# A recurrent mixing in log space: numerator, denominator and reciprocal replaced by a running mean with sigmoid weights

## What is computed

```
def step(carry, kv_t):
    p, q, o = carry
    no = maximum(o, u + kt);  A = exp(o - no);  E = exp(u + kt - no)
    y = (A * p + E * vt) / (A * q + E)
    no2 = maximum(w + o, kt); A2 = exp(w + o - no2); E2 = exp(kt - no2)
    return (A2 * p + E2 * vt, A2 * q + E2, no2), y
```

## Time and profile before

| | us |
|---|---|
| median of 3 runs | 2321.01 |
| lowest and highest | 2313.25, 2324.97 |
| profiled execution | 2336.95 |
| its span | 2335.2 |

### The profile page before, as it was taken

How to read it: one execution, slowest core, us unless ns; L and a number is a source line. 1 busy time by engine, 2 the same in 40 slices (tenths; PEclk the granted TensorE clock), 3 DMA queues, 4 the chain that set the end, 5 groups by cost and what they waited for, 6 DMA issues and landing times. The chain is left out here.

```text
span 2335.2 us, 36369 instructions
## 1 busy us (share of the span) xinstructions
PE 1755.0 (75%) x9338; PEld 1261.9 (54%) x9338; DVE 1225.8 (52%) x3526; ACT 762.4 (33%) x2164; POOL 1033.9 (44%) x1023
## 2 busy tenths in 40 slices
PE   7989946775569999999985655552177888888883
PEld 3566633443247777777753332322167677777762
DVE  3123343543334466666668777775334456666664
ACT  3312212111024454545443232222033333344341
POOL 5040043465713333333320566656655555555552
PEclk9989977887779999999996766665589999999996
DMA  9756557652246788776430263325745566777774
GB/s 304 215 125 159 145 179 260 256 175 79 99 146 224 250 277 284 282 278 226 150 138 27 98 238 110 107 92 192 265 133 149 150 204 226 236 239 239 242 241 175
DMA packets 244106, 444.72 MB, mean 190 GB/s; under 512 B 92561, under 2 KB 174609, under 8 KB 241169
## 3 DMA queue, kind: packets, MB, share of 16 engines
q1 hardware_dynamic: 168352, 237.46, 32.1%
q0 software_dynamic: 47856, 147.81, 17.7%
q10 hardware_dynamic: 27712, 57.28, 7.3%
HBM read 281.09 MB, written 237.60 MB: 222 GB/s over the span
## 5 line engine op out<-in xcount | busy, mean ns | idle before, releaser
L1041 PE MATMUL ps<-w_all,h_xT 128*128 x2112 | 557.2, 387 | 32.1 <-ACT h_xT L1312 21.1
L792 POOL DMA_INDIRECT y_b<-h_y,h_ix x314 | 313.3, 998 | 271.0 <-DVE h_y L1874 178.7
L1058 PE MATMUL ps<-w_all,h_hT 89*128 (+1 forms) x1472 | 413.1, 385 | 11.2 <-issue 6.1
L1041 PEld LDWEIGHTS ps<-w_all,h_xT 128*128 128x128 f32 x2112 | 346.8, 193 | 89.6 <-issue 42.9
L776 POOL DMA_INDIRECT xs_b<-h_x,slot_of x256 | 263.9, 1031 | 237.5 <-DVE slot_of L1705 162.0
L792 POOL DMA_INDIRECT y_a<-h_y,h_ix x208 | 201.6, 969 | 349.4 <-ACT h_y L1345 334.7
L1058 PEld LDWEIGHTS ps<-w_all,h_hT 89*128 89x128 f32 (+1 forms) x1472 | 269.1, 191 | 82.0 <-issue 26.8
L776 POOL DMA_INDIRECT xs_a<-h_x,slot_of x192 | 191.0, 995 | 194.1 <-DVE slot_of L1705 92.5
L1312 ACT COPY h_xT<-ps 128x256 f32<-128x256 f32 x528 | 195.0, 370 | 131.9 <-PE ps L1034 89.9
L1049 PE MATMUL ps<-ident,h_h 128*88 128x128 f32 (+1 forms) x736 | 170.1, 277 | 70.6 <-DVE h_h L1867 59.5
L1867 DVE TENSOR_TENSOR h_h<-ps,h_sg 128x96 f32<-128x96 f32 x320 | 81.8, 256 | 229.3 <-ACT h_sg L1322 198.6
(11 more groups left out here) (257 smaller groups left out, 2442.4 us busy)
## 6 DMA issues: line engine op xcount, KB each, us to landing
xs_b<-void_d SPq DMA_DIRECT2D x40, 1128.0 KB
h_x<-xs_b SPq DMA_DIRECT2D x80, 564.0 KB
h_c<-y_a ACTq DMA_DIRECT2D x28, 768.0 KB
h_x<-xs_a SPq DMA_DIRECT2D x34, 564.0 KB, 4.7
xs_a<-void_d ACTq DMA_DIRECT2D x16, 1128.0 KB
w_all<-in_exp SPq DMA_DIRECT2D x6, 2560.0 KB
h_x<-y_b SPq DMA_DIRECT2D x28, 512.0 KB
s_b<-y_b SPq DMA_DIRECT2D x28, 512.0 KB
```

The source lines that it names most:

```text
L792: pool.indirect_dma_start(y_d[L.name], bass.IndirectOffsetOnAxis(ap=h_ix[:, i % IX:i % IX + 1], axis=0), result_buffer(L, i), None).then_i ...
L1041: m = pe.matmul(ps[:, 2 + s % 2, 0:2 * L.H], h_xT[:, s % 2, c, :], w_all[:, bass.ds(e * L.W + c * 2 * L.H, 2 * L.H)], start=(c == 0), stop ...
L1058: m = pe.matmul(ps[:, 6 + s % 2, 0:D], h_hT[0:w, s % 2, j, :], w_all[0:w, bass.ds(e * L.W + L.up0 + j * D, D)], start=(j == 0), stop=(j == ...
```

## The change

The mixing is rewritten. With the logarithm of the running denominator, L = ln(q) + o, the mean m = p / q obeys m' = s m + (1 - s) v, with s the sigmoid of (w + L - k), and y = m + (v - m) sigmoid(u + k - L). The sigmoids are written as halves of 1 + tanh. The new lists:

- VectorE: `largest` is the scan of `w_o` alone, both halves at the head of the turn; `weight_sums` is the scan of the denominator `w_q`, both halves behind `residual`; `mixed` makes the keep factor `w_keep` by a tensor_scalar, `w_ev`, one scan `w_p`, and three more operations up to `w_y`. `w_max`, the two reciprocals, and the last multiplication are gone.
- ScalarE: two exponentials a half instead of four, then a logarithm of `w_q` a half (`logarithms`), and two tanh a half (`shares`), those of half 0 behind `rows_normalised`, those of half 1 behind `turned`.
- TensorE: two differences a half of two products, and one of three (`past_less_key`), which waits for the logarithm.
- Buffers of the stage grow by 44 floats per partition. The DMAs and the lists of SyncE and GpSimd are the same.

```
 PE
-            def differences(g, c):
...
+            def difference(n, plus, less):
+                if n >= 3:
+                    pe.wait_ge(wk_exp, n - 2)
+                for i, a in enumerate(plus):
+                    pe.matmul(ps[:, spread[n % 3], :], ident[:], a, start=(i == 0), stop=False)
+                pe.matmul(ps[:, spread[n % 3], :], minus[:], less, start=False, stop=True).then_inc(wk_less, 1)
+            def decays_of(g, c):
                 pe.wait_ge(wk_t, 2 * g + c + 1)
+                difference(6 * g + 2 * c, [w_o[:, c, :, 0:SEQ]], w_o[:, c, :, 1:SEQ + 1])
+                difference(6 * g + 2 * c + 1, [w_k[:, c, :, 1:SEQ + 1]], w_o[:, c, :, 1:SEQ + 1])
+            def past_less_key(g, c):
+                pe.wait_ge(wk_ln, 2 * g + c + 1)
+                difference(6 * g + 4 + c, [w_o[:, c, :, 0:SEQ], w_l[:, c, :, 0:SEQ]], w_k[:, c, :, 1:SEQ + 1])
...
-                    differences(g, 0)
-                    differences(g, 1)
+                    decays_of(g, 0)
+                    decays_of(g, 1)
+                    past_less_key(g, 0)
+                    past_less_key(g, 1)
 ACT
+            def logarithms(g, c):
+                act.wait_ge(wk_q, 2 * g + c + 1)
+                act.activation(w_l[:, c], w_q[:, c], ACT.Ln).then_inc(wk_ln, 1)
+            def shares(g, c):
+                src = of_bank(6 * g + 4 + c)
+                act.activation(w_tau[:, c, 1], src, ACT.Tanh, bias=w_half[:, c:c + 1], scale=0.5).then_inc(wk_tau, 1)
+                act.activation(w_tau[:, c, 0], src, ACT.Tanh, bias=w_half[:, KC + c:KC + c + 1], scale=0.5)\
+                   .then_inc(wk_exp, 1)
...
+                    logarithms(g, 0)
+                    logarithms(g, 1)
                 if g:
                     deviations(L1, g - 1)
                     rows_normalised(g - 1)
...
+                    shares(g, 0)
                     turned(L1, g - 1)
+                    shares(g, 1)
                     exponentials_of(L1, g - 1)
 DVE
+            def largest(g, c):
...
+                dve.tensor_tensor_scan(flat(w_o[:, c]), flat(w_dec[:, c]), flat(w_k[:, c]), 0.0, ALU.add, ALU.max)\
+                   .then_inc(wk_t, 1)
+            def weight_sums(g, c):
+                dve.drain()
+                dve.wait_ge(wk_exp, 6 * g + 2 * c + 2)
+                dve.tensor_tensor_scan(flat(w_q[:, c]), flat(w_a2[:, c]), flat(w_e2[:, c]), 0.0, ALU.mult, ALU.add)\
+                   .then_inc(wk_q, 1)
+            def mixed(g, c):
...
+                dve.wait_ge(wk_tau, 2 * g + c + 1)
+                dve.tensor_scalar(w_keep[:, c, :, 1:SEQ + 1], w_tau[:, c, 1], 0.5, 0.5, ALU.mult, ALU.add)
+                dve.scalar_tensor_tensor(w_ev[:, c, :, 1:SEQ + 1], w_tau[:, c, 1], 1.0, val, ALU.subtract, ALU.mult)
+                dve.drain()
+                dve.tensor_tensor_scan(flat(w_p[:, c]), flat(w_keep[:, c]), flat(w_ev[:, c]), 0.0, ALU.mult, ALU.add)
+                dve.drain()
+                dve.scalar_tensor_tensor(w_d[:, c], w_p[:, c, :, 0:SEQ], -0.5, val, ALU.mult, ALU.subtract)
+                dve.drain()
+                dve.wait_ge(wk_exp, 6 * g + 5 + c)
+                dve.scalar_tensor_tensor(w_d[:, c], w_tau[:, c, 0], 1.0, w_d[:, c], ALU.add, ALU.mult)
+                dve.drain()
...
+                m = dve.scalar_tensor_tensor(w_y[:, c], w_d[:, c], 0.5, val, ALU.mult, ALU.add)
...
             for g in range(NG + 1):
-                    exponents(g, 0)
+                    largest(g, 0)
+                    largest(g, 1)
                     slots_of(L1, g - 2)
                     residual(g - 1)
-                    exponents(g, 1)
-                    over_time(g, 0)
-                    denominators(g, 0)
+                    weight_sums(g, 0)
+                    weight_sums(g, 1)
                     row_scales(g - 1)
-                    over_time(g, 1)
+                    mixed(g, 0)
-                    denominators(g, 1)
                     less_largest(L1, g - 1)
-                    divided(g)
+                    mixed(g, 1)
                     chosen_experts(L1, g - 1)
```

More of the change, by code:

```diff
@@ L236, in flamingo @@
             w_e2 = s_("w_e2", [P, KC, GB, SEQ + 1])
-            w_ex = s_("w_ex", [P, KC, 2, GB, SEQ])
-            w_ev = s_("w_ev", [P, GB, SEQ + 1])
-            w_max = s_("w_max", [P, KC, GB, SEQ])
+            w_half = s_("w_half", [P, 2 * KC])
+            w_q = s_("w_q", [P, KC, GB, SEQ + 1])
+            w_l = s_("w_l", [P, KC, GB, SEQ + 1])
+            w_tau = s_("w_tau", [P, KC, 2, GB, SEQ])
+            w_keep = s_("w_keep", [P, KC, GB, SEQ + 1])
+            w_ev = s_("w_ev", [P, KC, GB, SEQ + 1])
             w_p = s_("w_p", [P, KC, GB, SEQ + 1])
-            w_q = s_("w_q", [P, KC, GB, SEQ + 1])
-            w_n = s_("w_n", [P, KC, GB, SEQ])
             w_d = s_("w_d", [P, KC, GB, SEQ])
-            w_m = s_("w_m", [P, GB, SEQ])
             w_y = s_("w_y", [P, KC, GB, SEQ])
@@ L354, in flamingo @@
         wk_exp = sem("wk_exp")
+        wk_q = sem("wk_q")
+        wk_ln = sem("wk_ln")
+        wk_tau = sem("wk_tau")
         wk_scale = sem("wk_scale")
@@ L1999, in flat @@
                 return ap.rearrange("p b t -> p (b t)")
-            def exponents(g, c):
+            def largest(g, c):
                 dve.drain()
@@ L2031, in over_time @@
-                dve.drain()
-                dve.tensor_tensor(w_n[:, c], w_n[:, c], w_m[:], ALU.add)
-            def denominators(g, c):
-                dve.drain()
-                dve.reciprocal(w_d[:, c], w_d[:, c])
-            def divided(g):
-                dve.drain()
-                if g:
-                    dve.wait_ge(wk_yt, g)
-                for c in range(KC):
-                    m = dve.tensor_tensor(w_y[:, c], w_n[:, c], w_d[:, c], ALU.mult)
-                m.then_inc(wk_y, 1)
+                    dve.drain().then_inc(wk_y, 1)
@@ L2059, in _ @@
                 dve.memset(w_a2[:, c, :, 0:1], 0.0)
-                dve.memset(w_e2[:, c, :, 0:1], 0.0)
-            dve.memset(w_ev[:, :, 0:1], 0.0)
-            dve.memset(w_max[:], 1.0)
+                dve.memset(w_e2[:, c, :, 0:1], 1.0)
+                dve.memset(w_keep[:, c, :, 0:1], 0.0)
+                dve.memset(w_ev[:, c, :, 0:1], 0.0)
+            dve.memset(w_y[:], 1.0)
             dve.wait_ge(wk_in, 48)
+            dve.tensor_scalar(w_half[:, 0:KC], w_wu[:, 0:KC], 0.5, None, ALU.mult)
+            dve.tensor_scalar(w_half[:, KC:2 * KC], w_wu[:, KC:2 * KC], -0.5, None, ALU.mult)
             dve.tensor_scalar(minus[:], ident[:], -1.0, None, ALU.mult)
@@ L2066, in _ @@
             for c in range(KC):
-                dve.tensor_scalar(w_dec[:, c, :, 1:SEQ + 1], w_max[:, c], w_wu[:, c:c + 1], None, ALU.mult)
+                dve.tensor_scalar(w_dec[:, c, :, 1:SEQ + 1], w_y[:, c], w_wu[:, c:c + 1], None, ALU.mult)
             dve.drain()
```

47 lines of the change are left out of this document (13 added, 34 removed).

## The result

| first chip | before | changed |
|---|---|---|
| median | 2320.72 (4 runs) | 2360.86 (4 runs) |
| lowest, highest | 2313.25, 2324.97 | 2337.46, 2791.51 |
| ratio of the comparable runs | | 1.012, 95% interval 1.0073 to 1.0167 |
| profiled execution | 2336.95 | 2366.82 |

The run of 2791.51 us, with a granted clock of 0.618 where the others have 0.86, is left out of the ratio. I had said 2299 and faster.

What follows compares the result with a forecast made beforehand. VectorE's chain was taken to set the 52.25 us turn, above GpSimd's 43.1 floor. Savings of 17.5 us (turns 3 to 7), 6 (turn 0) and 1.5 (turn 1), less 3 (turn 2), gave 22 off 2321: 2299, range 2270 to 2330.

Steps and rivals of the forecast that it cites:

- The sum on VectorE: VectorE's operations per turn: 17.9 us go, 6.9 come, 11.0 less by durations, 9.7 less after dependent starts.
- The tensor_scalar: VectorE's new operation in each half: 0.45 us; if each waits out a GpSimd instruction of 0.97, a turn loses 1.9.
- The waits for the root and the tanh: VectorE waiting for ScalarE each turn: root 2.3 us, adding 1.2; first tanh 4.2, before `mixed` of half 0.
- the drain: Rival, chance 0.03: 1380 ns of drain behind each ScalarE table load, some 2.8 us a turn, giving 2313 us.
- Turns 0 and 1: The stage's first turns: turn 0 ends at 27.2 us, 6 less; turn 1 takes 1.5 less.
- The wait for the logits: VectorE waiting for TensorE's gate product: 0.8 us added a turn, ends 0 and 4.7, from TensorE's list and clock.
- the pauses of 7.2 us a turn: VectorE's pauses in `chosen_experts` with no named releaser, while GpSimd issues DMAs; forecast to stay near 7 us.
- Turn 2: The stage's turn 2: loses 3 us, as transposes start later and half the mixing comes after `less_largest`.
- The pauses tied to GpSimd's run: Rival, chance 0.2: VectorE's choice ends with GpSimd's issues whatever comes before; a turn stays 52.6 us, total 2316.
- The slower one: Rival, chance 0.13: new VectorE waits catch pauses of 4.9 us, two a turn; a turn is 58.5, total 2348.
- The one on the pauses giving way: Rival, chance 0.14: VectorE's waits replace the pauses, GpSimd sets a turn of 43.3 us; 50 off, total 2271.

Runs made afterwards that it cites:

- h2: The changed kernel with less_largest held until GpSimd has issued 24 of 32 DMAs (the hold took effect earlier), slow chip: 2351.22 us, 1.0144 of the kernel before.
- s1: The changed kernel with GpSimd waiting after 12 of a group's 32 DMAs until VectorE has done less_largest, slow chip: 2280.78 us, 0.9977 of the kernel before.
- s2: The kernel before without its 16 wide reciprocals (division left out), slow chip: 2292.5 us, 1.0011 of the kernel before.
- h3: The changed kernel with mixed(g, 1) ahead of less_largest, and the same hold as h2, slow chip: 2341.07 us, 1.0076 of the kernel before.
- w1: The changed kernel with TensorE's past_less_key(g, 1) moved behind the transposes and gate product, slow chip: 2323.82 us, 1.0159 of the kernel before.
- the quiet window: The changed kernel with GpSimd waiting after 12 of 32 DMAs until less_largest is done: 0.9977 of the kernel before on a slow chip, 0.9994 on a fast one.

## Why the prediction was wrong, point by point

- **The sum on VectorE** was right. A half was costed at 5.1 us of `mixed` and takes 4.8; the scans stay at 1.242 us; scalar_tensor_tensors take 0.693, not 0.752; VectorE is busy 83 us less over the span (1225.8 to 1142.7 by the pages; 88 forecast).
- **The tensor_scalar** was costed at 0.45 with 0.97 as its bound; its mean is 0.481 and its longest 0.618 (0.651 on a fast chip, where the mean is higher too). By the rule of the Trainium skill that I set against it (SBUF — State Buffer, "Who interferes with whom") it could have waited out a whole GpSimd instruction; in the traces it lost 0.2 us at most, where one issue takes 0.97.
- **The waits for the root and the tanh**: 2.3 and 4.2 forecast, 2.15 and 4.22 or 4.23 measured in turns 2 to 7, and over the stage the same on both kinds of chip (15.7 and 35.6 us on the first, 15.7 and 35.4 on a fast one). The table load stays at 1283 ns and the first tanh starts 1.30 us after the load does: the drain of the Trainium skill (ScalarE: Activation LUTs, "What ACT_TABLE_LOAD costs") does not appear.
- **Turns 0 and 1**: 27.2 and 36.7 forecast, 28.8 and 35.5 measured.
- **The wait for the logits is the step that failed.** I wrote "I take 0.8, with ends 0 and 4.7", worked out from TensorE's list and clock. TensorE did its part within what I had forecast (the six products 7.4 us, from 1421.58 to 1428.97, between my 5.2 and 11; the gate product 3.67). The signal then took 10 us and more to arrive, which is in no row that I had priced: 12.6 to 22.3 us a turn on the first chip, waited by VectorE in turns 2 to 7. With it goes the assumption that the pauses of 7.2 us a turn would stay as they were.
- **Turn 2** was to lose 3 us and loses 10.6, by the same wait (17.8 us in it). On the fast chip, without that wait, it loses 2.9.
- **The rivals.** The pauses tied to GpSimd's run (0.2) had the right partner, and a turn of 52.6 us. In the kernel before, the next turn's first scan does start 0 to 4.9 us after the last issue; in the changed one it starts 5.0 to 14.6 after it, so a turn is 57 us and more. The slower one (0.13) had the mechanism nearly right: a new place at which VectorE waits catches a pause of its own. It put 4.9 us at two places and got 2348; in fact one place catches 12 to 22, in part in place of the old pauses (34.0 to 11.0), and the root and the tanh catch none. That its 2348 lies near the 2361 measured is in part luck. The one on the pauses giving way (0.14) had its turn of 43.3 us right, but on the fast chips: 43.2 to 44.1 there in four turns, then 41.0 to 43.0. It brings 9 us and not 50, because the kernel before has no pauses there either, and stands at 44 to 46.

What is shown: the sign goes with the kind of chip (five comparisons and h2, two kinds); on slow chips the wait that the forecast missed lies between the end of TensorE's work and the receiver's start, and in the turns read here it is over before GpSimd's run of issues or a few us behind it (1.4 to 4.0 in s1, 3.6 in turn 2 of the changed kernel); with GpSimd made to pause, the changed kernel is 41 us faster on the same chip (s1), though GpSimd does the same work; a like saving on VectorE without the new chain gains nothing there either (s2); the order on VectorE is worth some 10 us (h3), that on TensorE nothing (w1). What stays open is why the changed kernel ends 30 us behind s2, what holds these signals while GpSimd issues, why a signal sent in the kernel before at the same point of the run is often in time, and what sets the chips apart; every run here is a recorded one, so whether the recording has a part in it can't be told. No version beat the kernel before on both kinds: the quiet window is level with it on both (0.9977 and 0.9994), the changed kernel wins 0.5% on one and loses 1.3% on the other.

## What to carry to other kernels

Idle time that the trace gives to nobody ("issue", "remote") is not a constant to be carried through a sum: making an engine earlier moves it to the next signal, and it can grow there. Ask where the faster engine will first have to wait for another, and what else runs at that moment. Measure a change of one per cent on more than one chip: here its sign depended on it. And look in the trace whether a hold put into an experiment takes effect where it was meant to.
